# A decoder layer on one core: sixteen loads of the attention's folded weights issued by another engine

## What is computed

```python
x = x + mamba(_layernorm(x))        # W_in, causal conv of 4 taps, silu, W_x -> B and C, W_dt -> dt, scan, gate, W_out
x = x + cross(_layernorm(x), ctx)   # q = (x hW + hb) qW + qb; k, v from ctx through cW and kW, vW; softmax; oW, ob
x = x + experts(_layernorm(x))      # 8 experts, the best 2 of a token weighted by a softmax
```

## Time and profile before

| | us |
|---|---|
| three timed runs | 1502.41, 1504.59, 1505.41; median 1504.59 |
| the profiled execution, its own time | 1504.71 |
| its span, from first to last instruction | 1502.9 |
| DVE busy | 1327.0 (88%) |
| PE busy | 1218.4 (81%) |
| ACT busy | 999.3 (66%) |
| POOL busy | 949.9 (63%) |

### The profile page before, as it was taken

How to read it: one execution, slowest core, us unless ns; L and a number is a source line. 1 busy time by engine, 2 the same in 40 slices (tenths; PEclk the granted TensorE clock), 3 DMA queues, 4 the chain that set the end, 5 groups by cost and what they waited for, 6 DMA issues and landing times. The chain is left out here.

```text
span 1502.9 us, 22669 instructions
## 1 busy us (share of the span) xinstructions
PE 1218.4 (81%) x6134; PEld 853.0 (57%) x6134; DVE 1327.0 (88%) x1744; ACT 999.3 (66%) x1475; POOL 949.9 (63%) x522
## 2 busy tenths in 40 slices
PE   5978887689788888899788888899677777786897
PEld 2446664575555555685555555586355455575565
DVE  5479999888999999988899999988999999974687
ACT  5755554447978878837877877837777777732654
POOL 1379998514799889614798988723598988731000
PEclk9989998699899999999799999999789989897799
DMA  8112231421222212422121222512111112210111
GB/s 258 65 63 57 84 95 32 142 85 59 71 56 71 74 59 91 157 71 80 50 78 56 83 65 70 175 46 80 47 60 47 59 57 62 89 57 29 57 57 56
DMA packets 88013, 114.54 MB, mean 76 GB/s; under 512 B 9964, under 2 KB 62965, under 8 KB 87934
## 3 DMA queue, kind: packets, MB, share of 16 engines
q1 hardware_dynamic: 83836, 110.86, 23.5%
q10 hardware_dynamic: 4098, 2.74, 0.6%
HBM read 88.85 MB, written 24.73 MB: 76 GB/s over the span
## 5 line engine op out<-in xcount | busy, mean ns | idle before, releaser
L1827 DVE TENSOR_TENSOR_SCAN work<-ps,work 128x1024 f32<-128x1024 f32 x192 | 438.1, 2283 | 27.0 <-ACT ps L1299 24.9
L2413 PE MATMUL ps<-ident,work 128*128 128x128 f32 x1536 | 296.1, 314 | 163.4 <-DVE stage L1875 56.0
L1299 ACT ACTIVATE ps<-dt,a_neg 128x1024 f32<-128x1024 f32 x256 | 284.9, 1116 | 124.8 <-DVE work L1827 81.4
L2413 PEld LDWEIGHTS ps<-ident,work 128*128 128x128 f32 x1536 | 187.0, 156 | 287.4 <-DVE stage L1875 113.3
L887 POOL TENSOR_TENSOR work<-dtu,b_bc 128x1024 f32<-128x1024 f32 x124 | 290.2, 2369 | 44.4 <-PE ps L2413 43.2
L1875 DVE SCALAR_TENSOR_TENSOR stage<-ps,c_tok,stage 128x512 f32<-128x512 f32 x360 | 254.4, 733 | 9.7 <-PE ps L2413 8.2
L2435 PE MATMUL ps<-w,work 128*128 (+1 forms) x1024 | 250.0, 389 | 2.8 <-DVE work L2009 2.0
L2435 PEld LDWEIGHTS ps<-w,work 128*128 128x128 f32 x1024 | 195.9, 196 | 40.4 <-issue 4.1
L2385 PE MATMUL ps<-nfT,w 128*128 128x512 bf16 x512 | 163.6, 415 | 26.0 <-DVE work L1945 14.6
L887 POOL TENSOR_TENSOR work<-dtu,w_out 128x1024 f32<-128x1024 f32 x64 | 149.3, 2353 | 40.4 <-PE ps L2413 40.4
L906 POOL TENSOR_TENSOR stage<-stage,work 128x512 f32<-128x512 f32 x120 | 150.2, 1275 | 37.8 <-ACT work L1322 37.8
(11 more groups left out here) (189 smaller groups left out, 1921.8 us busy)
## 6 DMA issues: line engine op xcount, KB each, us to landing
b_bc<-b_rows SPq DMA_DIRECT2D x32, 512.0 KB, 4.8
w_out<-b_rows SPq DMA_DIRECT2D x32, 512.0 KB, 4.5
wbc<-combine_rows SPq DMA_DIRECT2D x64, 256.0 KB, 4.0
work<-z_rows SPq DMA_DIRECT2D x8, 1024.0 KB, 7.6
dtu<-conv_rows SPq DMA_DIRECT2D x12, 512.0 KB, 6.3
conv_rows<-mix SPq DMA_DIRECT2D x20, 256.0 KB, 2.8
stage<-in_x SPq DMA_DIRECT2D x8, 512.0 KB, 5.5
z_rows<-mix SPq DMA_DIRECT2D x16, 256.0 KB, 2.8
```

The source lines that it names most:

```text
L1299: act.activation(decay_in(d, alone, opening), dt[:, d, :], ACT.Exp, scale=a_neg[:, bass.ds(it * 2 + (d * N + hf * (N // 2) + par), 1)]).th ...
L1827: dve.tensor_tensor_scan(h, decays, h, 0.0, ALU.mult, ALU.add).then_inc(scan_done, 1)
L2413: mm = pe.transpose(ps[:, a % HT_BANKS, d * P:(d + 1) * P], slot(par, d)[:, a * P:(a + 1) * P], ident[:, :])
```

## The change

The sixteen `dma_start` calls leave ACT's stream, where they stood before all its computing, and stand in SP's stream, behind SP's nineteen loads and before its `phases`. Their order, sizes, targets and semaphore are the same.

```diff
@@ sync engine, behind the load of norm_w (L582)
+            for dst, name in ((qwT, "qWT"), (cwT, "cWT"), (kwT, "kWT"), (vwT, "vWT"), (owT, "oWT")):
+                sp.dma_start(dst, t[name].rearrange("(k p) f -> p k f", p=P)).then_inc(w_fold, 16)
+            sp.dma_start(hwb[:, :, 0:D], t["hW"].rearrange("(k p) f -> p k f", p=P)).then_inc(w_fold, 16)
+            sp.dma_start(hwb[:, :, D:D + 1], t["hb"].rearrange("(k p o) -> p k o", p=P, o=1),
+                         allow_slow_non_contiguous=True).then_inc(w_fold, 16)
+            for k in range(DK):
+                for c in range(2):
+                    sp.dma_start(ctxT[k][c], t["ctxT"][k * P:(k + 1) * P, c * KCH:(c + 1) * KCH]).then_inc(w_fold, 16)
+            for i, name in enumerate(("qb", "cb", "kb", "vb")):
+                sp.dma_start(fbias[:, i, :], t[name].rearrange("(k p) -> p k", p=P),
+                              allow_slow_non_contiguous=True).then_inc(w_fold, 16)
+            sp.dma_start(ob_row, t["ob"].rearrange("(a f) -> a f", a=1)).then_inc(w_fold, 16)
@@ scalar engine, ahead of scale_weights (L952 to L963)
-            for dst, name in ((qwT, "qWT"), (cwT, "cWT"), (kwT, "kWT"), (vwT, "vWT"), (owT, "oWT")):
-                act.dma_start(dst, t[name].rearrange("(k p) f -> p k f", p=P)).then_inc(w_fold, 16)
...
-            act.dma_start(ob_row, t["ob"].rearrange("(a f) -> a f", a=1)).then_inc(w_fold, 16)
```

## The result

| | before | changed |
|---|---|---|
| runs of the first comparison, us | 1506.01, median of 6 (1502.41 to 1507.92) | 1497.66, median of 6 (1494.82 to 1502.34) |
| ratio, 95% interval | | 0.995 (0.9931 to 0.9969) |
| second comparison, on another occasion | 1505.92, median of 23 | 1501.15, median of 12 (1498.11 to 1506.48) |
| ratio, 95% interval | | 0.997 (0.9957 to 0.9982) |
| profiled execution: own time, span | 1504.71, 1502.9 | 1499.04, 1496.9 |

The changed kernel is faster, by 8.4 us in the medians of the first comparison and by 4.8 in those of the second. The intervals of the two ratios overlap from 0.9957 to 0.9969, which is 4.7 to 6.5 us. The forecast was 5.3 us and 1499.4; the range from 1496.5 to 1503.0 holds both medians.

A forecast was written before the change was run, and what follows sets the result against it. DVE is busy 88% of the span, but ACT's sixteen DMA issues hold the start. Earlier scaling 4.59 plus x's landing 0.7 gives 5.3 us, other terms nothing: 1504.71 to 1499.4, range 1496.5 to 1503.0.

The forecast's parts named there:

- signs it named: Table load near 1 us, scaling 9.3 to 10.3, projections 15 to 16.2, B and C 38 to 38.9.
- ACT's issues: Kernel start: 12.54 us of issues leave ACT; scaling then waits for DVE's shift, starting at 10.23, not 14.82: 4.59 us.
- The table load: ACT before scaling: does not wait for its activation's semaphore, runs near 1 us, costs nothing; other end 1.28 given back.
- x's landing: Kernel start: x lands earlier without ACT's loads beside it; 0.7 us taken, bounds nothing to 1.0.
- The first weights: Before the projections: D_skip, landing at 16.94, expected before 14 and costed at nothing; bound 1.5 us given back.
- 3.7 us rival: First weights bind: projections start at 17.0, gain 3.7 us, 1501.0; 7% together with the table load binding.
- Row 1's statistics: DVE before the convolution: row 1's x gains by the same relief, 1.85 us idle there; cost nothing.
- SP: Sixteen issues added behind SP's nineteen end at 35, between 34.0 and 41.9; at 35 they cost nothing, 4 us cover.
- deadline of 39.2: SP's next work: gate store at 38.6 in the new time, plus 0.6 us free before the first softplus.
- has more air: SP's deadline: B's path has more slack than softplus's, since POOL's second product waits for DVE and not for B.
- The fold: Its loads land some 33 to 45 us later; first reader stands behind row 0's phase; cost nothing.
- last rival: Pipeline gives it back: shifted start may change where PE runs at its lower level; losing 3 us gives 1502.4; 9%.

The follow-up runs named there:

- run with seven loads: Changed kernel with the first seven of the sixteen loads (1.5 MB) back on ACT before the norm; 1502.82 us, ratio to before 0.9974.
- run with tiny issues: Changed kernel plus thirty 1 KB DRAM-to-DRAM copies issued on ACT where the sixteen loads stood; 1517.49 us, ratio to before 1.0073.
- second pair of traces: Both kernels rerun unaltered: before 1505.68 us, ratio to itself 1.0001; changed 1501.15 us, ratio 0.997.
- 32 and 14 tiny on SP: Changed kernel plus 32 or 14 1 KB copies on SP behind the sixteen loads; 1516.85 us, ratio to before 1.0067, and 1502.97 us, 0.9972.
- loads later; with the shift earlier: Changed kernel, sixteen loads behind B's stores and broadcast loads on SP: 1501.98 us, 0.9972 to before; additionally DVE's first-half shift earlier: 1500.89 us, 0.9965.

## Why the prediction was right

The direction, the place and the size held, and so did the signs it named, but for B and C, which begin at 37.90 and not between 38 and 38.9. Step by step:

1. **ACT's issues.** 4.59 was forecast from the shift as it stood. The scaling did start 0.03 behind the shift's end (9.20 + 0.16, then 9.39). The run with seven loads shows that issues are free which end a table load before the shift, the run with tiny issues that those beyond it are paid almost in full.
2. **The table load** ran at 0.95, as argued from silu's load.
3. **x's landing.** 0.47 earlier for the first half; and the second half's statistics, which waited until 0.44 behind the start of the instruction before them (0.27 of it idle), now begin 0.08 behind it: together 0.84 on the shift (10.04 to 9.20), where I took 0.7 out of 0 to 1.0. In the second pair of traces it is 1.10. The run with seven loads gives 0.70 of it back. Over all ten traces x lands at 4.64 to 4.89 without ACT's loads and at 5.35 to 5.61 with them. By the rule of the Trainium skill, "DMA: Bandwidth & Descriptors", section "Queues, rings and completion order", each DMA engine takes turns between the queues that have work. The traces agree as far as they go: x lands 0.46 us or more later where ACT's queue holds these loads.
4. **The first weights** landed at 10.1. The 3.7 us rival needed 16.9; it falls.
5. **Row 1's statistics** bound nothing: DVE idles 1.64 before the convolution.
6. **SP.** I took 35 and gave 34.0 to 41.9; it was 32.19, below my lower end. The term that was off is the price of an issue: 12.54 for sixteen was read from ACT's stream while SP issued beside it, where one of them took 2.43, and they take 8.2 on SP, at most 0.64 each. What stretches single issues there was not separated. The relief of SP's own loads was 5.35 and not 7.9. The deadline of 39.2 was near: the runs put it at 39.3 to 39.9, though by B's path and not by softplus's. That B's path "has more air" was wrong: the earlier trace rows have POOL idle 0.79 us before its second product, hardly more than softplus's 0.6, and in the changed kernel it is 0.47. Neither error touched the forecast, since 6 us of idle lay in between. The Trainium skill, "Perfetto Trace Analysis", section "DMA Optimizations", advises to spread issues over the engines where generating descriptors is the bottleneck. Here that is not so before SP's own deadline: with SP idle for 6 us behind the sixteen issues, moving them off ACT gained.
7. **The fold** waited for nothing.

Steps 1 and 3 come to 5.43 at the scaling. The first scan gained 5.65 in this pair of traces, and 61.21 - 55.46 = 5.75 in the other, against 5.3 forecast. The remaining 0.22 is a term that the sum did not have: TensorE's clock rose earlier within the projections (0.73 us for the first one before, 0.51 in the changed kernel; 0.38 for the first three in the second pair). By the repeats this moves from trace to trace, so I count it as chance. The span fell by 6.0 and by 2.4 in the same pairs, the medians by 8.4 and 4.8. What lies between is the body, from the first scan to the end. Mean clock and span (the view of cores), beside the length of that body (span less first scan):

| trace | clock | span | body |
|---|---|---|---|
| before, 1st and 2nd | 0.927, 0.932 | 1502.9, 1500.9 | 1442.1, 1439.7 |
| changed, 1st and 2nd | 0.929, 0.929 | 1496.9, 1498.5 | 1441.8, 1443.0 |
| seven loads on ACT | 0.926 | 1501.7 | 1445.8 |
| tiny on ACT | 0.922 | 1516.4 | 1448.2 |
| 32 and 14 tiny on SP | 0.921, 0.925 | 1513.7, 1500.9 | 1445.0, 1444.1 |
| loads later; with the shift earlier | 0.923, 0.925 | 1502.5, 1500.1 | 1448.0, 1445.7 |

All ten run the same body. It takes 1440 to 1443 us where the mean clock is 0.927 or more, and 1444 to 1448 where it is lower. This is the prediction's last rival, with its mechanism right and its sign open: the scatter of the body is as large as the whole effect, and it goes with the clock. That a lower clock makes PE's work longer, and not a longer body the mean clock lower, is shown only for the stretch from 738 to 774 us; whether a given start makes a given clock was not tried.

The timed executions say the same, since the mean clock of each is on record: 68 of the kernel before (all but those of the first comparison) and the 18 of the changed one. A straight line through both, with the same slope, gives 0.59 us more for each 0.001 less of clock. At equal clock the changed kernel is 5.8 us faster (95% interval 5.0 to 6.5). That fits the gain at the first scan, 5.65 and 5.75 less the 0.3 outside the span, and leaves nothing for the body that is told from zero. It also says where the two comparisons part: the changed kernel's executions had 0.929 on average in the first and 0.925 in the second, the kernel before 0.927 in the second. So the 8.4 us were in part a lucky clock. That 5.3 lies near what the change is worth is owed to its two terms, of which the second was 0.14 short; two small ones that it lacked, 0.22 from the clock's rise and 0.3 outside the span, go against each other.

## What to carry to other kernels

A DMA issue is an instruction of the engine that makes it, and in front of the first piece of an engine's work it is on the path even when nobody waits for its data; the profile shows it as "issue" and not as a wait, so look there. Before moving a list of loads, find the engine's next deadline on either side: here ACT's issues were free up to about 8 us (the shift's end at 9.4 less 1.28 for the table load) and SP's up to 38 or 39, and the same sixteen loads cost 5.7 us at the first scan on the one and nothing on the other. Where an effect is a few tenths of a per cent, measure it at a mark right behind the change and compare the timed runs at equal clock, not by their medians alone.

## What the runs showed of the hardware that was not expected

A copy of 1 KB from DRAM to DRAM took 0.65 to 0.68 us to issue (9.07 for 14, 20.41 for 30), while a load of 256 KB into 128 partitions took 0.47 on the same SP, and the load of the very same 1 KB (ob) into the core's own memory 0.33: the issue's price does not follow the bytes.

The second gate store's issue takes 0.62 us in the first trace of before and with the tiny copies on SP, and 1.85 to 2.58 in the others, the second trace of before among them (2.19), with the same instruction behind the same 1 MB gate store. Together with its landing this makes softplus wait up to 0.38 us. The position of the sixteen loads doesn't decide it; what does was not found.
